# Moving the last steps of the third and the last sequence, and fewer filler matmuls, in a Mamba-2 and mixture-of-experts kernel

## The reference

```python
h = rmsnorm(layernorm(x), norm1_w);  zxbcdt = h @ in_proj_w          # z, xBC, dt
xBC = silu(dw_causal_conv(xBC, conv_w, conv_b)); dt = softplus(dt + dt_bias)
y = ssd(xs, dt, -exp(A_log), Bm, Cm) + D * xs                        # chunks of 128 tokens
y = rmsnorm(y * silu(z), mixer_norm_w)
h1 = res + y @ out_proj_w
h2 = rmsnorm(h1, norm2_w)
mlp = silu(h2 @ gate_w) * (h2 @ up_w) @ down_w                       # 704 hidden columns
x = x + h1 + mlp
...
n = layernorm(x); p = softmax(n @ router_w)                          # 8 experts
top2 weights and indices of p, weights normalized
x = x + sum over the two experts e of w_e * (silu(n @ w1[e]) * (n @ w3[e])) @ w2[e]
```

## Time and profile before

| | us |
|---|---|
| median of 3 runs | 725.72 |
| lowest and highest | 724.36, 727.06 |
| the profiled execution, as timed | 726.26 |
| its span in the trace | 724.4 |
| PE busy in it | 692.7 (96%) |
| DVE busy | 581.6 (80%) |
| ACT, POOL busy | 240.8, 223.6 |

### The profile page before, as it was taken

One profiled execution on the slowest core, in us unless ns is written; L12 is line 12 of the kernel. 1 busy time (PEld: TensorE's weight loads), 2 busy tenths in 40 slices (PEclk: granted clock), 3 DMA queues, 4 the chain that ended last, 5 costly groups with the idle time before them and its releaser, 6 DMA issues.

```text
span 724.4 us, 10151 instructions
## 1 busy us (share of the span) xinstructions
PE 692.7 (96%) x2843; PEld 444.1 (61%) x2844; DVE 581.6 (80%) x1471; ACT 240.8 (33%) x487; POOL 223.6 (31%) x380
## 2 busy tenths in 40 slices
PE   5989999999999989999989999999999999999995
PEld 4457665558656766775865666666665555555563
DVE  3899999877866574476768888888888888988882
ACT  1576766585477435323121111111111111111110
POOL 2132322413221241220020333333333343434333
PEclk8999999999999999999999999999999999999999
DMA  9232002000220064033117891111151534434112
GB/s 317 64 117 89 30 1 85 34 1 1 70 106 0 1 210 153 1 92 120 33 51 253 278 300 29 26 27 28 29 178 34 149 64 122 97 90 130 30 22 30
DMA packets 39351, 63.22 MB, mean 87 GB/s; under 512 B 5456, under 2 KB 29072, under 8 KB 39312
## 3 DMA queue, kind: packets, MB, share of 16 engines
q1 hardware_dynamic: 31824, 52.61, 21.0%
q0 software_dynamic: 7488, 10.11, 8.8%
HBM read 52.88 MB, written 9.83 MB: 87 GB/s over the span
## 4 chain that ended last, share of the span: by engine, by line
PE 78%; DVE 11%; DMA 3%; issue 3%; ACT 2%; POOL 2%; POOLq 0%; DVEq 0%
PE ps L1110 23%; PE ps L1131 12%; PE ps L800 5%; PE ps L774 4%; PE ps L786 4%; PE ps L460 4%; PE ps L515 4%; PE ps L1119 3%; PE ps L582 3%; PE ps L639 3%; PE ps L529 3%; DMA out_rows<-big 2%; DVE big L1681 2%; DVE big L2313 2%; DVE big L1701 1%
## 5 line engine op out<-in xcount | busy, mean ns | idle before, releaser
L2313 DVE STREAM_TRANSPOSE big<-big 32x224 f32<-32x224 f32 x560 | 225.5, 403 | 8.4
L1110 PE MATMUL ps<-big 128*128 x512 | 198.6, 541 | 1.3 <-ACT big L1583 0.7
L1110 PEld LDWEIGHTS ps<-big 128*128 128x128 f32 x512 | 96.3, 190 | 88.0 <-issue 86.4
L1131 PE MATMUL ps<-big 128*128 x448 | 102.2, 380 | 1.0 <-DVE big L2313 0.6
L1589 ACT ACTIVATE big<-ps 128x896 f32<-128x896 f32 x36 | 33.0, 917 | 200.8 <-PE ps L1110 177.5
L1131 PEld LDWEIGHTS ps<-big 128*128 128x128 f32 x448 | 82.6, 190 | 11.7 <-issue 1.8
L2365 POOL TENSOR_TENSOR big<-big 128x1 f32<-128x1 f32 x110 | 22.0, 200 | 176.9 <-DVE big L2303 153.4
L460 PEld LDWEIGHTS ps<-big 128*128 128x128 f32 x319 | 39.9, 145 | 38.7 <-issue 27.6
L460 PE MATMUL ps<-big 128*128 128x128 f32 x319 | 52.4, 279 | 8.1 <-DVE big L1764 2.3
L2553 POOL DMA_INDIRECT out_rows<-big x32 | 51.3, 1603 | 18.2 <-issue 18.2
L1681 DVE SCALAR_TENSOR_TENSOR big<-ps,big 128x511 f32<-128x511 f32 (+2 forms) x72 | 53.0, 747 | 4.3 <-ACT big L1236 2.3
(11 more groups left out here) (246 smaller groups left out, 1019.7 us busy)
## 6 DMA issues: line engine op xcount, KB each, us to landing
big<-in_w SPq DMA_DIRECT2D x36, 896.0 KB, 7.8
big<-cum_rows SPq DMA_DIRECT2D x16, 512.0 KB, 5.7
out_rows<-big SPq DMA_DIRECT2D x4, 512.0 KB, 2.9
xn_rows<-big SPq DMA_DIRECT2D x4, 512.0 KB, 3.1
big<-in_hidden SPq DMA_DIRECT2D x1, 1536.0 KB, 12.3
big<-in_in_proj SPq DMA_DIRECT2D x1, 1288.0 KB, 7.1
big<-in_gate SPq DMA_DIRECT2D x1, 640.0 KB, 13.2
big<-in_up SPq DMA_DIRECT2D x1, 640.0 KB, 8.7
```

The source lines that it names most:

```text
L1110: last = mm(bank(bk + n)[:, 0:HALF], xT[:, k, :], expert_cols(e, off + k * M + n * HALF, HALF), start=(k == 0), stop=(k == KD - 1))
L1131: last = mm(bank(7)[:, 0:D], hTs[:, half, j * P:(j + 1) * P], expert_cols(e, 2 * KD * M + j * D, D), start=(j == 0), stop=(j == MB - 1))
L2313: last = V.transpose(hTs[c * SQ:(c + 1) * SQ, half, :].rearrange("p (j t) -> p j t", j=MB)[:, :, q * SQ:(q + 1) * SQ], ha[q * SQ:(q + 1) * ...
```

## The change

Nothing is computed in another way, and no instruction is added; steps are moved within the list of their engine, and 6 of 8 fillers are gone. Two waits of PE change with the order: `out_` of the last sequence's third chunk no longer waits for the copy of the logits of sequence 1, and `logits(1, 1)` waits for the last `h1_` of sequence 3, since it now stands behind the last `out_`.

```diff
-WARM_START, WARM_LAST, WARM_PLACE, WARM_ROWS = 5, 8, 5, 6
+WARM_START, WARM_LAST, WARM_PLACE, WARM_ROWS = 5, 2, 5, 6
...
-                elif c == 2 and n >= 2:
-                    pe.wait_ge(lg_taken, n - 1)
+                elif c == 2 and n == 2:
+                    pe.wait_ge(lg_taken, 1)
...
-                    pe.wait_ge(o_taken, nth(n + 2, CH, part))
+                    pe.wait_ge(o_taken, nth(n + 2, CH, part if n == 0 else CH - 1))
```

On PE, end of sequence 2:

```diff
             mlp_down(1, 1)
+            yT_(2, 3)
             mlp_down(1, 2)
-            yT_(2, 3)
+            out_(2, 3)
             mlp_down(1, 3)
 
             diag(3, 0)
-            out_(2, 3)
-
-            diag(3, 1)
+
             state_(3, 0)
             h2T_(2)
+            diag(3, 1)
             off_(3, 1)
```

On PE, end of sequence 3:

```diff
             out_(3, 1)
+            diag(3, 3)
             mlp_down(2, 0)
-
-            diag(3, 3)
+            yT_(3, 2)
+
             mlp_down(2, 1)
-            yT_(3, 2)
-            logits(1, 1)
-            mlp_down(2, 2)
             out_(3, 2)
             yT_(3, 3)
+            mlp_down(2, 2)
+            out_(3, 3)
             mlp_down(2, 3)
-            out_(3, 3)
+            logits(1, 1)
             keep_warm(DIAG, WARM_LAST)
             h2T_(3)
+            mlp_gate(3, 0)
+            mlp_up(3, 0)
             positions(1)
             xnT_(2, 0)
-            mlp_gate(3, 0)
-            mlp_up(3, 0)
             mlp_gate(3, 1)
```

On ACT:

```diff
             square_h(2, 0)
+            yT_copy(2, 3)
 
             front(3, 1)
             square_h(2, 1)
             square_h(2, 2)
-            yT_copy(2, 3)
             square_y(2, 3)
...
             gate(2, 4)
+            x_D(3, 3)
             xnT_copy(1, 1)
             square_h(3, 0)
             gate(2, 5)
-            x_D(3, 3)
-            logits_copy(1)
...
             square_h(3, 3)
+            logits_copy(1)
             h2T0(3)
```

On DVE, end of sequence 2:

```diff
             add_mlp(1, 2)
+            h1_(2, 3)
             route_next(0)
             add_mlp(1, 3)
             ln2_stats(1)
 
+            h2(2)
             y_(3, 0)
-            h1_(2, 3)
             xn_(1)
-            h2(2)
             state(3, 0)
```

On DVE, end of sequence 3:

```diff
             add_mlp(2, 0)
-            route_pick(1)
             h1_(3, 2)
+            add_mlp(2, 1)
             route_rec(0)
-            add_mlp(2, 1)
+            h1_(3, 3)
             add_mlp(2, 2)
+            h2(3)
             add_mlp(2, 3)
             ln2_stats(2)
-            h1_(3, 3)
+            h2T1(3)
+            route_pick(1)
+            xn_(2)
             route_next(1)
-            h2(3)
-            xn_(2)
-            h2T1(3)
             route_place(0)
```

On POOL:

```diff
             scale_y(2, 3)
-            ln2_scale(1)
             scaled_x(3, 1)
             scale_h(2)
+            ln2_scale(1)
             decayed_x(3, 1)
...
             scale_y(3, 3)
+            scale_h(3)
             ln2_scale(2)
-            scale_h(3)
```

## The result

| | before | changed |
|---|---|---|
| median, 8 runs each, us | 724.11 | 720.70 |
| lowest and highest | 722.88, 727.06 | 718.40, 721.37 |
| the profiled execution, as timed | 726.26 | 720.28 |
| its span | 724.4 | 718.4 |

By the medians the changed kernel is 3.4 us faster. The ratio, which is taken over all runs and isn't that of the medians, is 0.994, with a 95% interval of 0.992 to 0.996: 4.3 us, 2.9 to 5.8. The two profiled executions lie 6.0 us apart. The forecast was 721.8, with 4.5 us of gain. So the time came out 1.1 lower than forecast, while the gain is 1.1 smaller than the sum by the medians, 0.2 smaller by the ratio, and 1.5 larger between the traces. What lies between these numbers is the subject of the experiments.

A forecast was written before the change was run, and what follows sets the result against it. PE, 78% of the span, was taken as the bound, so only its waits and slow clock pay. Gains of 3.4 and 1.1, together 4.5 us, off the profiled 726.26 gave 721.8 us, range 720.1 to 724.8.

The forecast's parts named there:

- End of sequence 2: From `mlp_down(1, 3)` to `mlp_gate(2, 0)`: less waiting and half clock on PE, gain 3.4 us, bounds 1.8 to 4.0.
- the new wait: PE ahead of `off_(3, 1)`: waits about 0.6 us for DVE's `state(3, 0)`.
- the part that is only waiting: Before `mlp_gate(2, 0)`: 1.8 of the 3.4 us gain comes from waits, not from clock.
- POOL's shadow: At `h2(2)` and `h1_(2, 3)`: a POOL step slows DVE; `h2` 1.15 instead of 1.92 us, `h1_` perhaps 0.3 slower.
- End of sequence 3: From the last `out_` to `mlp_gate(3, 2)`: `mlp_down(2, 3)`, `logits(1, 1)` and six fillers leave the way; gain 1.1 us.
- The wait for `hidden_(3, 0)`: PE ahead of `mlp_gate(3, 2)`: stands about 1.5 us until DVE's list reaches that product.
- Rival 2: DVE isn't late at the sequence 3 end, which gains 2.8 us; time 720.1, chance 0.09.
- Rivals 3 and 5: Sequence 3 end gives nothing, 722.9 to 723.6, chance 0.13; the second, `h2T_(3)` still waits for `h2(3)`, is part of it.
- 1.6 us of half clock: At `h2T_(2)`: the share of the 3.4 us gain that comes from PE running at full clock.
- rival 1: At `h2T_(2)`: the clock gives less, no fall or one in both kernels; gain 2.9 us, time 723.4, chance 0.28.
- rival 4: At the removed fillers and new waits: clock falls of about 1.7 us each make it slower, 727.9; chance 0.05.

The follow-up runs named there:

- b1: The kernel before, unchanged, run again for a second look; timed 723.44 us.
- e4: The changed kernel with `slots(0)` and `slots(1)` on DVE each moved behind the `hidden_` product that followed; median 721.93 us, ratio to before 0.9944.
- b2: The kernel before, unchanged, run again for a third look; timed 724.24 us.
- e2: The changed kernel with the end of sequence 2 put back as before, so only the sequence 3 end changed, with two fillers; 723.29 us, ratio to before 0.9973.
- e3: The changed kernel with `xn_(1)` on DVE moved behind `state(3, 0)` and `h2T1(2)`; median 721.12 us.
- e7: The changed kernel with 3 fillers added in two PE waits at the tail; runs from 720.03 to 723.45 us.
- e5: The changed kernel with 8 fillers again instead of 2; `mlp_gate(2, 0)` to `mlp_gate(3, 2)` took 63.12 us.
- e6: The changed kernel with none of the two remaining fillers; median 720.86 us.
- e10: The changed kernel with `xn_(1)` behind `h2T1(2)`, both `slots` behind their `hidden_` products and no fillers; median 718.60 us, ratio to before 0.9916.
- e1: The kernel before with the change at the end of sequence 2 alone, 8 fillers kept; 722.76 us, ratio to before 0.9965.

## Why the prediction was right or wrong

**End of sequence 2: right.** `h2T_(2)` was put at 259.3 in the old time and came at 259.27 (259.08 + 0.19); the new wait at 0.6 and is 0.70. The gain was put at 3.4 and is 3.19; the part that is only waiting at 1.8, and against b1 it is 1.78 (26.37 - 24.59). `y_`'s second pass took 1.00, not the 0.68 that I took from a row of another kind, yet this isn't what makes the 0.2: `h2` was a little early and DVE's rows overlap, so `state(3, 0)` ended only 0.06 later than in the sum. `off_` started another 0.06 behind it and took 1.13, not 1.02. I looked for POOL's shadow on `h2` and on `h1_`, and it fell on `y_`: `decayed_x(3, 1)` had moved beside it. The Trainium skill's rule (SBUF — State Buffer, "Who interferes with whom") covers this case, two operands in SBUF beside a GpSimd step. `h1_`'s L1758, for which I had named it, took 0.42: it started at 254.45, and `scaled_x(3, 1)` had ended at 254.24, so the two never met.

**End of sequence 3: right in kind, 0.4 too small.** The wait for `hidden_(3, 0)` is there, with 0.96 where I had 1.5, and the gain is 1.52 where I had 1.1; 0.10 is given back before `mlp_down(3, 0)`, so 1.4. PE came to `h2T_(3)` 0.2 earlier than in my sum, and DVE's list from `h2T1(3)` to the end of `hidden_(3, 0)` took 10.14, not 10.23. Rival 2, with 2.8, has fallen: e4 shows that DVE holds PE. Rivals 3 and 5 have fallen too: this end gives 1.4, and `h2(3)` was ready 0.5 before PE came to `h2T_(3)`, as said. The step `positions(1)` waits 0.17, as said.

**The clock: this is the step that failed.** I took 1.6 us of half clock from one trace into the sum, as if every execution had it, and costed everything behind 340 us at nothing. The first is a fall that costs 1.41 and stands in three of the four traces that have the hole (before, b2 and e2, not b1). The second, 0.98 at the tail, was in the trace of before and by chance not in that of the changed kernel. Between the two traces, clock and start explain the 6.0: 3.2 of moves (1.78 + 1.52 - 0.10), 1.41 and 0.98 of falls, and 0.4 of scatter at both ends. The base had the same error. The profiled execution of before, 726.26, has both falls and lies 2.15 above the median of 8 runs, 724.11; I saw 0.54 of this and didn't take it off. An execution with more falls than usual is the wrong base for a sum of waits. That 721.8 came within 1.1 of the measured 720.7 is luck: the base was 2.15 too high, and the gain, by the medians, 1.1 too large.

What the clock gives on average stays open. The moves give 3.2. The medians' 3.4 leaves next to nothing for it, the ratio's 4.3 leaves 1.1, and three falls in four of 1.41 each would be 1.06, an estimate from few traces. Both lie in the interval of 2.9 to 5.8, and so does rival 1, which had 2.9 for the gain and which I ranked below the forecast. Its time, 723.4, was wrong like mine, since I set it against 726.26; 724.11 less 2.9 is 721.2. Its other half, a fall in the changed kernel too, is in none of the eight traces with the new order at this place.

**Slower by falls at the removed fillers (rival 4): real, but small.** In none of the five traces with two fillers there (the changed kernel, e2, e3, e4 and e7) did the clock fall at `mlp_gate(3, 0)`; in one of the two with none it did, for 1.18 of the stage. With the two fillers, waits of up to 0.96 brought none. The row of the Trainium skill (TensorE: Matmul & The Clock Gate, "Why this matters for your kernels") that I had named for this rival warns of longer gaps than these, so it was no argument for it. The two fillers left in may be worth their 0.3 us; two traces don't settle it.

**What stays open.** The stage up to `mlp_gate(1, 5)` takes 237.7 to 240.5 us with the same instructions, nearly as much as the whole effect of the change. Much of this goes with the clock at the start. From 12 to 22 us the mean granted clock is 0.83 in four traces (b2, e2, e4, e5), and they take 237.7 to 237.9; it is 0.66 in eight others, and they take 239.1 to 240.5. Of these eight, the two at 240.5 (e3, e6) have a fall near 120 us, the one at 239.1 (e10) has none in this stage but the one at the start, and the other five, like the first four, have one near 48. Why the start differs, I can't say.

The record of the clock isn't complete. In e7's trace it shows 1.00 where the same transposes take 1.97 instead of 1.09 us, as at half clock (first e7, then the changed kernel):

```profile
11.33 1.97 PE L460 MATMUL ps<-big 128*128 128x128 f32 x8 [0.68 <-DVE big L1643]
```

```profile
11.26 1.09 PE L460 MATMUL ps<-big 128*128 128x128 f32 x8 [0.86 <-DVE big L1641]
```

In the kernel before, five fillers take 4.63 us at the start and 2.32 later, and the record shows 1.00 for both:

```profile
6.00 4.63 PE L808 MATMUL ps<-big 128*128 128x256 f32 x10 [6.00 <-DMA big<-in_vecs]
366.46 2.32 PE L808 MATMUL ps<-big 128*128 128x256 f32 x10
```

So the mean granted clock of an execution isn't a full count of its falls. How often each fall comes in untraced executions is open too.

## What to carry to other kernels

Cut the span at fixed steps of the engine that bounds it and compare stages, not totals: most stages without a clock change repeat to 0.02 us, while single executions of one kernel lie up to 5 us apart (the 24 of before beside e1: 721.98 to 727.21). Before a stretch at half clock goes into a sum, look at a second and a third execution, and keep what it costs apart from the waits, in the gain and in the base alike. When steps are moved behind the one that was late, add up the moved ones on their engine up to the next result that somebody waits for: that turned 2.8 us into 1.5 here, and moving one step of 1.2 us on won 1.1 of it back.

## What the runs showed of the hardware

In the thirteen traces the granted clock falls at a few places, most of them in part of the executions only, between its levels of 2.4 and 1.2 GHz. It falls at the start (in all but e7, where the record shows nothing), near 48 us (9 traces), near 120 (2), at the hole near 262 (3 of the 4 that have it), near 314 (e10), between 350 and 360 (6), between 371 and 376 (3), and in the last 3 to 5 us (all). A fall cost 1.41 at `h2T_(2)`, 0.98 at the tail, 1.18 at `mlp_gate(3, 0)`, and 1.9 to 2.7 in the first expert tiles (354.96 and 355.68 against 353.02). The Trainium skill (TensorE: Matmul & The Clock Gate, Part 1) says that the point of the change differs from run to run. The three traces of the unchanged kernel agree: from 14 to 16 us the mean granted clock is 0.59, 0.64 and 1.00. They also show more than that: at the same hole of 1.6 us a fall comes or doesn't.

A DVE step and a POOL step can slow each other. The four steps of `h2` take 1.91 us beside a POOL step 512 wide (L2398, from 261.46) and 1.14 beside one 4 wide. The second pass of `y_` takes 1.00 in the changed kernel, where L2398 started 0.58 ahead of it. In the kernel before it takes 0.69 and starts 0.11 ahead of the POOL step L2391, which then takes 1.49, against 1.12 in the changed kernel.
